# Three weight buffers instead of two, and the second layernorm applied by halves, in a transformer layer on eight cores

## The chip, the cores and the metric

The kernel runs on all 8 cores of one Trainium2 chip. Each core computes one of the eight batch elements from its own copy of x and the same weights; the cores do not exchange anything. The metric is the device time of one launch in microseconds, that of the slowest core.

## What is computed

One pre-norm transformer layer on x of shape (8, 2048, 1024) in float32, with 16 heads of 64 in the attention and a feed-forward part of four hidden products, cut here to its core:

```python
x = x + attn(layernorm(x), wq, bq, wk, bk, wv, bv, wo, bo)   # softmax attention, 16 heads
n = layernorm(x)                                             # over the last axis, eps 1e-5
h = silu(n @ w1.T * s1) * (n @ w2.T * s2)                    # 1024 -> 4096
h = gelu(h @ h1.T * sh1)                                     # 4096 -> 4096
h = gelu(h @ h2.T * sh2)                                     # 4096 -> 4096
x = x + (h @ w3.T * s3)                                      # 4096 -> 1024
```

The change touches the second layernorm and the feed-forward part.

## The kernel before

Everything lies with features on the 128 partitions and the S = 2048 tokens of the core's batch element along the free dimension. KD = 8 chunks of 128 features make up D = 1024, KH = 32 make up the 4096. The program is a row of blocks written out by hand. In a block each engine has its own queue of instructions in program order, and semaphores order the engines (a count that an instruction raises by `then_inc`, and that another engine awaits by `wait_ge`). Between blocks all engines meet at a barrier.

First come the first layernorm and the projections with the attention (to about 1029 us), then the normalisation of the attention, the product with wo, whose result x2 lies in x2buf in float32 and is stored to x2hbm, and the statistics of the second layernorm: the rows of means and of inverse deviations, both in rowbuf2, one partition each. The change begins behind them.

**Second layernorm, application (lines 932 to 957).** A block of its own. TensorE spreads the row of means and the row of inverse deviations over all partitions: four matmuls of 512 columns each with a column of ones, into ps_mrep (line 939) and ps_rrep (line 943). Each takes 4 of the 8 PSUM banks. Then VectorE subtracts and multiplies for each of the 8 chunks k, over all 2048 tokens, from x2buf through xsq2 (float32) into act_bf (bfloat16): 16 operations. They go through the helper vop (line 191 in the profile), which makes each wait for the one before.

**Feed-forward part (lines 959 to 1102).** The list sched holds the units of work. There are two halves of the tokens (hf = 0, 1; THALF = 1024 tokens each). In each half come 32 units of w1, 32 of w2, 32 of h1, 32 of h2 and 8 of w3, so 136 units in a half and 272 in all. A unit i computes 128 output features for 1024 tokens: 16 matmuls of 128x512 for w1 and w2 (8 chunks of input by 2 column blocks), and 64 for h1, h2 and w3. Its weights, 128 x 1024 or 128 x 4096 values, are loaded by POOL's queue from float32 in HBM into bfloat16 in wb0 or wb1, by turns. Its result goes into one of two halves of ps_f.

- POOL (line 992) waits until unit i - 2 is through, then issues the load for unit i (line 993). The loads of units 0 and 1 are issued ahead, in the block of the wo product (lines 798, 799).
- TensorE (line 1022) waits for the load and for the eviction of unit i - 2. At the first unit of each stage (m == 0) it waits for all evictions so far, since every unit of a stage reads all that the stage before wrote.
- ScalarE evicts w1 (silu, into hbufA), h1 (gelu, into hbufA) and h2 (gelu, into hbufB) on line 1042; VectorE evicts w2 (times hbufA, into hbufB, line 1058) and w3 (plus x2, into ostg, line 1069).
- SyncE loads x2 back for w3 and stores the output.

hbufA takes the first 64 KB per partition of the arena. It lies over xsq2 (0 to 16 KB), rowbuf2 (16 to 32 KB) and the first half of x2buf (from 32 KB). Each eviction writes 2 KB of it, so the one of unit m = 8 is the first to write where rowbuf2 was, and that of m = 16 the first where x2buf was. The x2 store has to be through before the evictions begin (s_x2st).

```python
g.wait_ge(s_mm, mm0 + i - 1)
g.dma_start(wb[i % 2][:, 0: kc * 128], src[m]).then_inc(swl[i % 2], 16)
```

Of the kernel before, what the change touches and what calls it, by code (L numbers as in the profile page):

```python
# [6 lines left out]
F32 = mybir.dt.float32  # L7
BF16 = mybir.dt.bfloat16
# [4 lines left out]
B, S, D, H, E, HID = 8, 2048, 1024, 16, 64, 4096  # L13
KD = D // 128
KH = HID // 128
# [35 lines left out]
    "ostg":    (139264, 8192),  # L51
    "wb0":     (148352, 8192),
    "wb1":     (156544, 8192),
}
ARENA_SIZE = 164736


def build_nc():
    nc = bass.Bass("TRN2", target_bir_lowering=False)
# [50 lines left out]
    def arena(name, shape, dtype):  # L110
        off, sz = AR[name]
        esz = 2 if dtype == BF16 else 4
        nbytes = int(np.prod(shape[1:])) * esz
        assert nbytes <= sz, (name, nbytes, sz)
        return nc.alloc_sbuf_tensor_at(name, shape, dtype,
                                       offset=arena_base + off)[:]
# [27 lines left out]
    hbufB = arena("hbufB", [128, KH * THALF], BF16)  # L144
    wb0 = arena("wb0", [128, KH * 128], BF16)
    wb1 = arena("wb1", [128, KH * 128], BF16)
    x2rb = arena("x2rb", [128, 2 * 1024], F32)
    ostg = arena("ostg", [128, 2 * 1024], F32)

# [4 lines left out]
    with es:  # L154
# [10 lines left out]
        s_dcp = es.enter_context(nc.semaphore("s_dcp"))  # L165
        s_wl0 = es.enter_context(nc.semaphore("s_wl0"))
        s_wl1 = es.enter_context(nc.semaphore("s_wl1"))
        s_wc = es.enter_context(nc.semaphore("s_wc"))
        s_mm = es.enter_context(nc.semaphore("s_mm"))
        s_evs = es.enter_context(nc.semaphore("s_evs"))  # L170
# [10 lines left out]
        s_xe = es.enter_context(nc.semaphore("s_xe"))  # L181
        s_dd1 = es.enter_context(nc.semaphore("s_dd1"))

        swl = [s_wl0, s_wl1]
        sxr = [s_xr0, s_xr1]
        sout = [s_o0, s_o1]
        sdd = [s_dd0, s_dd1]
# [1 line left out]
        def vop(v, meth, *a, **kw):  # L189
            v.wait_ge(s_v, n["v"])  # L190
            getattr(v, meth)(*a, **kw).then_inc(s_v, 1)  # L191
            n["v"] += 1
            return n["v"]
# [102 lines left out]
        with nc.Block() as blk:  # L296
            @blk.gpsimd
            def _(g):
                g.dma_start(onescol_bf, onescol_c).then_inc(s_small, 16)
                g.dma_start(bqs, bq_d).then_inc(s_small, 16)  # L300
                g.dma_start(bks, bk_d).then_inc(s_small, 16)
                g.dma_start(bo_sb, bo_d).then_inc(s_small, 16)
                g.dma_start(bvr_sb, bv_d).then_inc(s_small, 16)
                g.dma_start(s1_sb, s1_d).then_inc(s_small, 16)
                g.dma_start(s2_sb, s2_d).then_inc(s_small, 16)
                g.dma_start(sh1_sb, sh1_d).then_inc(s_small, 16)
                g.dma_start(sh2_sb, sh2_d).then_inc(s_small, 16)
                g.dma_start(s3_sb, s3_d).then_inc(s_small, 16)
                g.wait_ge(s_x, 16)
                g.dma_start(wq_sb, wq_d).then_inc(s_wqkv, 16)  # L310
                g.dma_start(wk_sb, wk_d).then_inc(s_wqkv, 16)
                g.dma_start(wv_sb, wv_d).then_inc(s_wqkv, 16)
# [475 lines left out]
        with nc.psum_tensor("ps_sxb", [1, S], F32) as ps_sxb:  # L788
            with nc.psum_tensor("ps_wo", [128, 2 * 1024], F32) as ps_wo:
                with nc.Block() as blk:  # L790
# [4 lines left out]
                    @blk.gpsimd  # L795
                    def _(g):
                        g.wait_ge(s_pe, pe0 + 2 * KD + KD - 1)
                        g.dma_start(wb0[:, 0: KD * 128], w1_d[0]).then_inc(s_wl0, 16)
                        g.dma_start(wb1[:, 0: KD * 128], w1_d[1]).then_inc(s_wl1, 16)

                    @blk.sync
                    def _(sy):
# [122 lines left out]
                        vop(v, "tensor_scalar", rowr, rowr, -0.5, 1.5, ALU.mult, ALU.add)  # L925
                        vop(v, "tensor_mul", rowr, rowt, rowr)

        with (
            nc.psum_tensor("ps_mrepb", [128, S], F32) as ps_mrep,
            nc.psum_tensor("ps_rrepb", [128, S], F32) as ps_rrep,  # L930
        ):
            with nc.Block() as blk:
                @blk.tensor
                def _(t):
                    rowm = rowbuf2[0:1, 0:S]
                    rowr = rowbuf2[0:1, S:2 * S]
                    ins = None
                    for nn in range(4):
                        t.matmul(ps_mrep[:, nn * 512:(nn + 1) * 512], ones_sb,
                                 rowm[0:1, nn * 512:(nn + 1) * 512],  # L940
                                 start=True, stop=True)
                    for nn in range(4):
                        ins = t.matmul(ps_rrep[:, nn * 512:(nn + 1) * 512], ones_sb,
                                       rowr[0:1, nn * 512:(nn + 1) * 512],
                                       start=True, stop=True)
                    ins.then_inc(s_pe, 1)

                n["pe"] += 1

                @blk.vector  # L950
                def _(v):
                    v.wait_ge(s_pe, n["pe"])
                    for k in range(KD):
                        vop(v, "tensor_sub", xsq2[:, (k % 2) * S:(k % 2) * S + S],
                            x2buf[:, k * S:(k + 1) * S], ps_mrep[:])
                        vop(v, "tensor_mul", act_bf[:, k * S:(k + 1) * S],
                            xsq2[:, (k % 2) * S:(k % 2) * S + S], ps_rrep[:])

        wb = [wb0, wb1]
        sched = []  # L960
        for hf in range(2):
            sched += [("w1", hf, m) for m in range(KH)]
# [18 lines left out]
        w3_evv_val = [evv0 + evv_b[i] + 1  # L981
                      for i, (lay, hf, m) in enumerate(sched) if lay == "w3"]

        with nc.psum_tensor("ps_f", [128, 2 * 1024], F32) as ps_f:
            with nc.Block() as blk:
                @blk.gpsimd
                def _(g):
                    for i, (lay, hf, m) in enumerate(sched):
                        if i < 2:
                            continue  # L990
                        src, kc = wsrc[lay]
                        g.wait_ge(s_mm, mm0 + i - 1)  # L992
                        g.dma_start(wb[i % 2][:, 0: kc * 128], src[m]).then_inc(swl[i % 2], 16)  # L993

                @blk.tensor
                def _(t):
                    for i, (lay, hf, m) in enumerate(sched):
                        src, kc = wsrc[lay]
                        t.wait_ge(swl[i % 2], 16 * (i // 2 + 1))
                        if m == 0:  # L1000
                            if evs_b[i] > 0:
                                t.wait_ge(s_evs, evs0 + evs_b[i])
                            if evv_b[i] > 0:
                                t.wait_ge(s_evv, evv0 + evv_b[i])
                        elif i >= 2:
                            lay2 = sched[i - 2][0]
                            if eng[lay2] == "s":
                                t.wait_ge(s_evs, evs0 + evs_b[i - 2] + 1)
                            else:
                                t.wait_ge(s_evv, evv0 + evv_b[i - 2] + 1)  # L1010
                        if lay in ("w1", "w2"):
                            rhs, rb, rstride = act_bf, hf * THALF, S
                        elif lay == "h1":
                            rhs, rb, rstride = hbufB, 0, THALF
                        elif lay == "h2":
                            rhs, rb, rstride = hbufA, 0, THALF
                        else:
                            rhs, rb, rstride = hbufB, 0, THALF
                        ins = None
                        for k in range(kc):  # L1020
                            for nn in range(2):
                                ins = t.matmul(  # L1022
                                    ps_f[:, (i % 2) * 1024 + nn * 512:(i % 2) * 1024 + (nn + 1) * 512],
                                    wb[i % 2][:, k * 128:(k + 1) * 128],
                                    rhs[:, k * rstride + rb + nn * 512: k * rstride + rb + (nn + 1) * 512],
                                    start=(k == 0), stop=(k == kc - 1))
                        ins.then_inc(s_mm, 1)
# [4 lines left out]
                @blk.scalar  # L1032
                def _(sc):
                    sc.wait_ge(s_x2st, 16 * KD)
                    for i, (lay, hf, m) in enumerate(sched):
                        if eng[lay] != "s":
                            continue
                        sc.wait_ge(s_mm, mm0 + i + 1)  # L1038
                        dst = hbufA if lay in ("w1", "h1") else hbufB
                        func = AF.Silu if lay == "w1" else AF.Gelu  # L1040
                        ssb = {"w1": s1_sb, "h1": sh1_sb, "h2": sh2_sb}[lay]
                        sc.activation(dst[:, m * THALF:(m + 1) * THALF],  # L1042
                                      ps_f[:, (i % 2) * 1024:(i % 2) * 1024 + 1024],
                                      func, scale=ssb[:, m:m + 1]).then_inc(s_evs, 1)
                        n["evs"] += 1
# [120 lines left out]
```

## Time and profile before

| | us |
|---|---|
| median of the two timed runs | 4099.9 |
| the two timed runs | 4070.94 and 4128.85 |
| the profiled execution, its own time | 3864.26 |
| its span on the slowest core, from the first to the last instruction | 3862.7 |

| stage in the profiled execution | from, us | to, us |
|---|---|---|
| rows of the second layernorm done | | 1249.9 |
| broadcasts and application of the second layernorm | 1250.2 | 1302.6 |
| w1 and w2, half 0 | 1303.0 | 1570.8 |
| h1, half 0 | 1576.6 | 2023 |
| h2 and w3, half 0 | 2023 | 2577 |
| w1 and w2, half 1 | 2579.2 | 2850.5 |
| h1, h2 and w3, half 1 | 2857.9 | 3862 |

PE is TensorE's matmuls, PEld its loads of weights, DVE is VectorE, ACT is ScalarE, SP is SyncE. PEclk and the granted clock are the share of TensorE's full speed of 2.4 GHz that the chip gave it. In a group the first number behind the bar is the busy time, then comes the mean of one instruction; behind the second bar stands the idle time of that engine just before these instructions, and what ended it. In the chain of waits each piece begins where the one before it ends, and "issue" is time in which nothing shown was waited for. Matmul records overlap, so a pitch is taken from a stretch divided by its count.

### The profile page before, as it was taken

What the parts mean: (1) busy time and instruction counts of PE and PEld (TensorE: products, weight loads), DVE (VectorE), ACT (ScalarE), POOL (GpSimd) and SP (SyncE); (2) the same over time, 40 slices, a digit from 0 to 9 for tenths busy, and PEclk for the clock granted to TensorE, in tenths of its full rate; (3) what the DMA queues carried; (4) which work ended last, traced back from release to release, by engine and by line L of the source; (5) the groups of instructions that cost most, each with busy time, mean ns of one, the idle gap of its engine ahead of it and who ended that gap; (6) DMA issues with size and microseconds to landing.
All of it is one profiled execution on the core that took longest, in us unless ns stands there. A gap on an engine that the chain in (4) does not pass through costs nothing.

```text
span 3862.7 us, 35099 instructions; the slowest of 8 cores (3845.2 to 3862.7 us)
## 1 busy us (share of the span) xinstructions
PE 3384.2 (88%) x14708; PEld 1385.2 (36%) x14708; DVE 479.1 (12%) x453; ACT 805.6 (21%) x741; POOL 151.3 (4%) x290
## 2 busy tenths in 40 slices
PE   2378888888696588999999999998889999999999
PEld 0122222222132233344444444443334444444444
DVE  0522222222222303000000000000210000000000
ACT  1014777777601120000000000002000000000000
POOL 0000000000000011000000000001100000000000
PEclk9589999999868799999999999999999999999999
DMA  6000000001013244444444444454444444444445
GB/s 153 0 1 1 1 1 1 1 1 23 1 62 118 33 63 64 80 76 76 76 76 73 77 76 76 96 127 63 63 74 77 77 77 77 75 76 76 76 71 144
DMA packets 49612, 237.44 MB, mean 61 GB/s; under 512 B 7777, under 2 KB 7842, under 8 KB 28338
## 3 DMA queue, kind: packets, MB, share of 16 engines
q0 software_dynamic: 40176, 193.04, 29.8%
q1 hardware_dynamic: 9282, 42.15, 3.1%
q8 instruction: 120, 1.97, 0.2%
q14 instruction: 34, 0.28, 0.0%
HBM read 411.19 MB, written 16.78 MB: 111 GB/s over the span
## 4 chain that ended last, share of the span: by engine, by line
PE 59%; DMA 5%; issue 1%; ACT 0%; DVE 0%; POOLq 0%; DVEq 0%; ACTq 0%
PE ps_f L1022 59%; DMA wb<-w 5%; DMA wb<-h 0%; ACT hbufA L1042 0%; DVE hbufB L1058 0%; DVE ostg L1069 0%; ACT hbufB L1042 0%; POOLq L992 0%; ACTq L1038 0%; DVEq L1056 0%; DVEq L1055 0%; DVEq L1068 0%; DVEq L1066 0%
## 5 line engine op out<-in xcount | busy, mean ns | idle before, releaser
L1022 PE MATMUL ps_f<-hbufB,wb 128*128 128x512 bf16 x5120 | 1110.8, 380 | 16.1 <-DMA wb<-h 13.2
L1022 PE MATMUL ps_f<-hbufA,wb 128*128 128x512 bf16 x4096 | 884.4, 379 | 3.0 <-ACT hbufA L1042 3.0
L1022 PEld LDWEIGHTS ps_f<-hbufB,wb 128*128 128x128 bf16 x5120 | 501.8, 98 | 625.1 <-issue 24.9
L728 ACT ACTIVATE pbuf<-ps_sc,cneg 128x1024 bf16<-128x1024 f32 x512 | 531.3, 1135 | 268.8 <-PE ps_sc L434 267.5
L1022 PEld LDWEIGHTS ps_f<-hbufA,wb 128*128 128x128 bf16 x4096 | 400.6, 98 | 486.8 <-issue 4.0
L1022 PE MATMUL ps_f<-act_bf,wb 128*128 128x512 bf16 x2048 | 457.4, 381 | 122.2 <-DMA wb<-w 62.1
L1022 PEld LDWEIGHTS ps_f<-act_bf,wb 128*128 128x128 bf16 x2048 | 194.8, 98 | 385.9 <-issue 168.6
L455 PE MATMUL ps_aE<-pbuf,vt_sb 128*65 128x512 bf16 x512 | 220.6, 431 | 86.5 <-DVE q_sb L712 85.3
L1069 DVE SCALAR_TENSOR_TENSOR ostg<-ps_f,s_sb,x2rb 128x1024 f32<-128x1024 f32 x16 | 20.6, 1284 | 1994.0 <-PE ps_f L1022 1994.0
L1042 ACT ACTIVATE hbufB<-ps_f,sh_sb 128x1024 bf16<-128x1024 f32 x64 | 71.4, 1116 | 816.0 <-PE ps_f L1022 816.0
L1042 ACT ACTIVATE hbufA<-ps_f,sh_sb 128x1024 bf16<-128x1024 f32 x64 | 71.4, 1116 | 784.7 <-PE ps_f L1022 784.7
L434 PE MATMUL ps_sc<-q_sb,k_sb 64*128 64x512 bf16 x1024 | 212.8, 406 | 18.6 <-ACT pbuf L728 1.5
L455 PE MATMUL ps_aO<-pbuf,vt_sb 128*65 128x512 bf16 x512 | 208.2, 407 | 0.0
L434 PEld LDWEIGHTS ps_sc<-q_sb,k_sb 64*128 64x128 bf16 x1024 | 58.6, 93 | 262.2 <-issue 262.1
L1058 DVE SCALAR_TENSOR_TENSOR hbufB<-ps_f,s_sb,hbufA 128x1024 bf16<-128x1024 f32 x64 | 82.2, 1284 | 460.5 <-PE ps_f L1022 460.5
L455 PEld LDWEIGHTS ps_aE<-pbuf,vt_sb 128*65 128x65 bf16 x512 | 56.7, 111 | 215.8 <-issue 215.8
L993 POOL DMA_DIRECT2D wb<-h x128 | 67.6, 528 | 1683.6 <-PE ps_f L1022 1651.6
L1042 ACT ACTIVATE hbufA<-ps_f,s_sb 128x1024 bf16<-128x1024 f32 x64 | 71.4, 1116 | 191.9 <-PE ps_f L1022 191.9
L1042 ACT ACT_TABLE_LOAD x4 | 5.1, 1283 | 493.9 <-PE ps_f L1022 493.9
L993 POOL DMA_DIRECT2D wb<-w x142 | 74.9, 528 | 804.1 <-PE ps_f L1022 804.1
L229 PE MATMUL ps_sxa<-xbuf,onescol_sb 128*1 128x512 f32 x64 | 30.6, 623 | 73.5 <-PEq L296 73.5
L771 PE MATMUL ps_rep<-rtile,selpair 16*128 16x512 f32 x64 | 54.9, 1058 | 17.0 <-DVE rtile L191 17.0
(93 smaller groups left out, 1003.2 us busy)
## 6 DMA issues: line engine op xcount, KB each, us to landing
wb<-h POOLq DMA_DIRECT2D x128, 1024.0 KB, 8.1
wb<-w POOLq DMA_DIRECT2D x128, 256.0 KB, 3.8
wb<-w POOLq DMA_DIRECT2D x16, 1024.0 KB, 9.5
xrb<-xst SPq DMA_DIRECT2D x8, 1024.0 KB, 4.8
x2hbm<-x2buf SPq DMA_DIRECT2D x8, 1024.0 KB, 14.2
x2rb<-x2hbm SPq DMA_DIRECT2D x16, 512.0 KB, 9.7
out_fm<-ostg SPq DMA_DIRECT2D x16, 512.0 KB, 8.9
wqld<-wq POOLq DMA_DIRECT2D x1, 2048.0 KB, 16.6
```

Of the source, the lines that this page charges most:

```text
L229: t.matmul(ps_sx[:, nn * 512:(nn + 1) * 512], onescol_sb, src[:, k * S + nn * 512: k * S + (nn + 1) * 512], start=(k == 0), stop=(k == KD ...
L434: ins = t.matmul(ps_sc[:, bufo + hh * TQ: bufo + (hh + 1) * TQ], k_sb[p0:p0 + 64, j * S + c * 128: j * S + (c + 1) * 128], q_sb[p0:p0 + 64 ...
L455: ins = t.matmul(ps_a[:, :], vt_sb[:, vslot: vslot + 65], pbuf[:, sb + hh * TQ: sb + (hh + 1) * TQ], start=(c == 0), stop=(c == TC - 1))
L728: sc.activation(pbuf[:, (c % 4) * 1024:(c % 4) * 1024 + 1024], ps_sc[:, (c % 2) * 1024:(c % 2) * 1024 + 1024], AF.Exp, bias=cneg[:, j:j + ...
L771: ins = t.matmul(ps_rep[:, (j % 2) * S + nn * 512:(j % 2) * S + (nn + 1) * 512], selpair_sb[:, j * 128:(j + 1) * 128], rtile[:, nn * 512:( ...
L993: g.dma_start(wb[i % 2][:, 0: kc * 128], src[m]).then_inc(swl[i % 2], 16)
L1022: ins = t.matmul(ps_f[:, (i % 2) * 1024 + nn * 512:(i % 2) * 1024 + (nn + 1) * 512], wb[i % 2][:, k * 128:(k + 1) * 128], rhs[:, k * rstri ...
L1042: sc.activation(dst[:, m * THALF:(m + 1) * THALF], ps_f[:, (i % 2) * 1024:(i % 2) * 1024 + 1024], func, scale=ssb[:, m:m + 1]).then_inc(s_ ...
L1058: v.scalar_tensor_tensor(hbufB[:, m * THALF:(m + 1) * THALF], ps_f[:, (i % 2) * 1024:(i % 2) * 1024 + 1024], s2_sb[:, m:m + 1], hbufA[:, m ...
L1069: v.scalar_tensor_tensor(ostg[:, (nst % 2) * 1024:(nst % 2) * 1024 + 1024], ps_f[:, (i % 2) * 1024:(i % 2) * 1024 + 1024], s3_sb[:, m:m + ...
```

## The change

Two things are changed.

**Three weight buffers.** wb2 joins wb0 and wb1, with a semaphore s_wl2 of its own. Unit i takes buffer i % 3, its load waits until unit i - 3 is through, and the loads of three units are issued ahead. The list of units, the two halves of ps_f and the evictions stay.

**Layernorm by halves.** The separate block for the application is gone; its work now stands at the head of the feed-forward block, for tokens 0 to 1023 and then for 1024 to 2047. Each half has 4 broadcast matmuls into ps_m2 and ps_r2 (2 banks each, so that they fit beside the 4 banks of ps_f) and 16 VectorE operations on 128x1024. The subtraction now writes act_bf in bfloat16, and the multiplication works in place there; xsq2 is not used for it. The broadcasts of half 1 wait for VectorE's last operation of half 0 (vnh[0]), because they overwrite the same banks. The first w1 unit of a half waits for that half's operations (vnh[hf]). ScalarE waits for the broadcasts of half 1 before the eviction of m = 8, and for the operations of half 1 before that of m = 16, because hbufA lies over rowbuf2 and x2buf.

```diff
@@ @@
                         g.dma_start(wb0[:, 0: KD * 128], w1_d[0]).then_inc(s_wl0, 16)
                         g.dma_start(wb1[:, 0: KD * 128], w1_d[1]).then_inc(s_wl1, 16)
+                        g.dma_start(wb2[:, 0: KD * 128], w1_d[2]).then_inc(s_wl2, 16)
...
-                @blk.vector
-                def _(v):
-                    v.wait_ge(s_pe, n["pe"])
-                    for k in range(KD):
-                        vop(v, "tensor_sub", xsq2[:, (k % 2) * S:(k % 2) * S + S],
-                            x2buf[:, k * S:(k + 1) * S], ps_mrep[:])
-                        vop(v, "tensor_mul", act_bf[:, k * S:(k + 1) * S],
-                            xsq2[:, (k % 2) * S:(k % 2) * S + S], ps_rrep[:])
...
+                for hf_ in range(2):
+                    @blk.tensor
+                    def _(t, hf=hf_):
+                        if hf == 0:
+                            t.wait_ge(s_v, vrows)
+                        else:
+                            t.wait_ge(s_v, vnh[0])
+                        ins = None
+                        for nn in range(2):
+                            t.matmul(ps_m2[:, nn * 512:(nn + 1) * 512], ones_sb,
...
+                        for nn in range(2):
+                            ins = t.matmul(ps_r2[:, nn * 512:(nn + 1) * 512], ones_sb,
...
+                        ins.then_inc(s_pe, 1)
+                        n["pe"] += 1
+                        pe_rep[hf] = n["pe"]
+
+                    @blk.vector
+                    def _(v, hf=hf_):
+                        v.wait_ge(s_pe, pe_rep[hf])
+                        for k in range(KD):
+                            vop(v, "tensor_sub",
+                                act_bf[:, k * S + hf * 1024: k * S + hf * 1024 + 1024],
+                                x2buf[:, k * S + hf * 1024: k * S + hf * 1024 + 1024],
+                                ps_m2[:])
+                            vop(v, "tensor_mul",
+                                act_bf[:, k * S + hf * 1024: k * S + hf * 1024 + 1024],
+                                act_bf[:, k * S + hf * 1024: k * S + hf * 1024 + 1024],
+                                ps_r2[:])
+                        vnh[hf] = n["v"]
...
-                        if i < 2:
+                        if i < 3:
                             continue
                         src, kc = wsrc[lay]
-                        g.wait_ge(s_mm, mm0 + i - 1)
-                        g.dma_start(wb[i % 2][:, 0: kc * 128], src[m]).then_inc(swl[i % 2], 16)
+                        g.wait_ge(s_mm, mm0 + i - 2)
+                        g.dma_start(wb[i % 3][:, 0: kc * 128], src[m]).then_inc(swl[i % 3], 16)
...
-                        t.wait_ge(swl[i % 2], 16 * (i // 2 + 1))
+                        t.wait_ge(swl[i % 3], 16 * (i // 3 + 1))
+                        if lay == "w1" and m == 0:
+                            t.wait_ge(s_v, vnh[hf])
...
+                        if lay == "w1" and hf == 0 and m == 8:
+                            sc.wait_ge(s_pe, pe_rep[1])
+                        if lay == "w1" and hf == 0 and m == 16:
+                            sc.wait_ge(s_v, vnh[1])
```

On TensorE, between the last matmul of the statistics and the fourth w1 unit, the queue before reads as follows (ps_mrepb and ps_rrepb are the spread rows):

```order
L889 MATMUL ps_sqb<-sqbf2_66,onescol_bf 1x512 x3
L872 UNCONDITIONAL_BRANCH
L933 UNCONDITIONAL_BRANCH [waits barrier_Pool_Activation_PE_DVE_SP_release]
L939 MATMUL ps_mrepb<-rowbuf2_67,ones_sb 128x512 x4
L943 MATMUL ps_rrepb<-rowbuf2_67,ones_sb 128x512 x4
L932 UNCONDITIONAL_BRANCH
L995 UNCONDITIONAL_BRANCH [waits barrier_Pool_Activation_PE_DVE_SP_release]
L1022 MATMUL ps_f<-act_bf,wb0_70 128x512 [waits s_wl0]
L1022 MATMUL ps_f<-act_bf,wb0_70 128x512 x15
L1022 MATMUL ps_f<-act_bf,wb1_71 128x512 [waits s_wl1]
L1022 MATMUL ps_f<-act_bf,wb1_71 128x512 x15
L1022 MATMUL ps_f<-act_bf,wb0_70 128x512 [waits s_wl0,s_evs]
```

And the same place in the changed kernel:

```order
L970 UNCONDITIONAL_BRANCH [waits barrier_Pool_Activation_PE_DVE_SP_release]
L978 MATMUL ps_m2<-rowbuf2_67,ones_sb 128x512 [waits s_v]
L978 MATMUL ps_m2<-rowbuf2_67,ones_sb 128x512
L982 MATMUL ps_r2<-rowbuf2_67,ones_sb 128x512 x2
L970 UNCONDITIONAL_BRANCH
L978 MATMUL ps_m2<-rowbuf2_67,ones_sb 128x512 [waits s_v]
L978 MATMUL ps_m2<-rowbuf2_67,ones_sb 128x512
L982 MATMUL ps_r2<-rowbuf2_67,ones_sb 128x512 x2
L1012 UNCONDITIONAL_BRANCH
L1041 MATMUL ps_f<-act_bf,wb0_70 128x512 [waits s_wl0,s_v]
L1041 MATMUL ps_f<-act_bf,wb0_70 128x512 x15
L1041 MATMUL ps_f<-act_bf,wb1_71 128x512 [waits s_wl1]
```

The eight broadcast matmuls are now two groups of four, each behind a wait for VectorE, and both stand ahead of the first w1 unit.

On POOL, before, the loads of the weights up to the second that waits for a unit:

```order
L798 DMA wb0_70<-w1 128x1024 [waits s_pe]
L799 DMA wb1_71<-w1 128x1024
L790 UNCONDITIONAL_BRANCH
L986 UNCONDITIONAL_BRANCH [waits barrier_Pool_Activation_PE_DVE_SP_gather]
L993 DMA wb0_70<-w1 128x1024 [waits s_mm]
L993 DMA wb1_71<-w1 128x1024 [waits s_mm]
```

And in the changed kernel:

```order
L801 DMA wb0_70<-w1 128x1024 [waits s_pe]
L802 DMA wb1_71<-w1 128x1024
L803 DMA wb2_72<-w1 128x1024
L793 UNCONDITIONAL_BRANCH
L1003 UNCONDITIONAL_BRANCH [waits barrier_Pool_Activation_PE_DVE_SP_gather]
L1010 DMA wb0_70<-w1 128x1024 [waits s_mm]
L1010 DMA wb1_71<-w1 128x1024 [waits s_mm]
```

Three loads stand ahead of the barrier instead of two, and those behind it go round three buffers.

## Rows read from the trace of the kernel before

**Rows 1.** Head of the page

```profile
span 3862.7 us, 35099 instructions; the slowest of 8 cores (3845.2 to 3862.7 us)
```

**Rows 2.** Granted clock: die, median span, mean granted clock

```profile
die 0 (median of its cores): 3851.5 us, clock 0.950
```

**Rows 3.** The chain that ended last, by line, share of the span

```profile
PE ps_f L1022 59%; DMA wb<-w 5%; DMA wb<-h 0%; ACT hbufA L1042 0%; DVE hbufB L1058 0%; DVE ostg L1069 0%; ACT hbufB L1042 0%; POOLq L992 0%; ACTq L1038 0%; DVEq L1056 0%; DVEq L1055 0%; DVEq L1068 0%; DVEq L1066 0%
```

**Rows 4.** Groups: busy, mean ns of one | idle before, releaser

```profile
L1022 PE MATMUL ps_f<-hbufB,wb 128*128 128x512 bf16 x5120 | 1110.8, 380 | 16.1 <-DMA wb<-h 13.2
...
L1022 PE MATMUL ps_f<-act_bf,wb 128*128 128x512 bf16 x2048 | 457.4, 381 | 122.2 <-DMA wb<-w 62.1
```

**Rows 5.** The chain in time, start of w1, half 0: start us, us, what

```profile
1303.04 5.05 PE ps_f L1022 x16
...
1308.62 3.84 DMA wb<-w
...
1312.71 3.63 PE ps_f L1022 x16
```

**Rows 6.** DMA issues: count, KB each, median us to landing

```profile
wb<-h POOLq DMA_DIRECT2D x128, 1024.0 KB, 8.1
```

**Rows 7.** Timeline of the layernorm's application: start us, us, engine, line, operation

```profile
1247.65 2.28 DVE L191 TENSOR_TENSOR rowbuf<-xsq,rowbuf 1x2048 f32<-1x2048 f32 x1
...
1250.25 7.16 PE L939 MATMUL ps_mrepb<-rowbuf,ones_sb 1*128 1x512 f32 x8 [22.75 <-PEq L872]
...
1264.41 2.29 DVE L191 TENSOR_TENSOR xsq<-x2buf,ps_mrepb 128x2048 f32<-128x2048 f32 x1 [14.48 <-PE ps_rrepb L943]
1266.80 2.29 DVE L191 TENSOR_TENSOR act_bf<-xsq,ps_rrepb 128x2048 bf16<-128x2048 f32 x1
```

**Rows 8.** VectorE groups before 1250 us, shapes apart; columns as in Rows 4

```profile
L191 DVE SCALAR_TENSOR_TENSOR x2buf<-ps_wo,bo_sb,xrb 128x1024 f32<-128x1024 f32 x16 | 20.5, 1284 | 61.4 <-PE ps_wo L831 61.4
...
L670 DVE TENSOR_TENSOR vt_sb<-ps_x,bvrep 128x1024 bf16<-128x1024 f32 x16 | 19.6, 1227 | 60.4 <-PE ps_x L413 60.4
L191 DVE TENSOR_TENSOR attn_n<-q_sb,ps_rep 128x2048 bf16<-128x2048 bf16 x8 | 18.3, 2288 | 39.4 <-PE ps_rep L771 39.4
```

**Rows 9.** Stretches: us, busy PE, PEld, DVE, ACT, POOL, PEclk, DMA share, GB/s

```profile
1250.30:1264.10 13.80, 13.80 (x16) 5.06 (x16) 0.00 (x0) 0.00 (x0) 0.00 (x0) 0.50 0.00 0
1303.00:1575.00 272.00, 228.50 (x1024) 97.45 (x1024) 41.08 (x32) 37.00 (x33) 33.77 (x64) 0.99 0.45 66
1576.00:2023.00 447.00, 445.06 (x2048) 200.97 (x2048) 0.00 (x0) 37.00 (x33) 16.88 (x32) 0.99 0.43 75
1576.50:1580.00 3.50, 3.44 (x9) 1.24 (x10) 0.00 (x0) 0.00 (x0) 0.00 (x0) 0.50 1.04 152
2023.00:2466.00 443.00, 442.19 (x2048) 200.32 (x2048) 0.00 (x0) 35.21 (x32) 16.55 (x32) 1.00 0.44 76
```

**Rows 10.** Landing of the loads into wb, w1 and w2 of half 1

```profile
DMA to landing us min/median/max: 3.6/3.9/5.7
```

**Rows 11.** The chain in time, into w2 (half 0) and w1 (half 1)

```profile
1438.23 0.02 issue
...
1439.58 7.08 PE ps_f L1022 x32
...
2579.15 3.63 PE ps_f L1022 x16
```

**Rows 12.** Timeline, first h1 matmuls of both halves; idle before in brackets

```profile
1576.56 23.76 PE L1022 MATMUL ps_f<-hbufB,wb 128*128 128x512 bf16 x96 [5.80 <-DMA wb<-h]
...
2857.86 12.33 PE L1022 MATMUL ps_f<-hbufB,wb 128*128 128x512 bf16 x46 [7.36 <-DMA wb<-h]
```

**Rows 13.** The two loads issued ahead

```profile
L798 POOL DMA_DIRECT2D wb<-w x1: 527/527/527, 1200.4 to 1200.4; - x1
...
DMA to landing us min/median/max: 8.9/9.2/9.6
```

More of the change, by code:

```diff
@@ L53 @@
     "wb1":     (156544, 8192),
+    "wb2":     (164736, 8192),
 }
-ARENA_SIZE = 164736
+ARENA_SIZE = 172928
 def build_nc():
@@ L146, in build_nc @@
     wb1 = arena("wb1", [128, KH * 128], BF16)
+    wb2 = arena("wb2", [128, KH * 128], BF16)
     x2rb = arena("x2rb", [128, 2 * 1024], F32)
@@ L167, in build_nc @@
         s_wl1 = es.enter_context(nc.semaphore("s_wl1"))
+        s_wl2 = es.enter_context(nc.semaphore("s_wl2"))
         s_wc = es.enter_context(nc.semaphore("s_wc"))
@@ L182, in build_nc @@
         s_dd1 = es.enter_context(nc.semaphore("s_dd1"))
-        swl = [s_wl0, s_wl1]
+        swl = [s_wl0, s_wl1, s_wl2]
         sxr = [s_xr0, s_xr1]
@@ L926, in _ @@
                         vop(v, "tensor_mul", rowr, rowt, rowr)
[L928 to L948, printed above, removed]
-                @blk.vector
-                def _(v):
-                    v.wait_ge(s_pe, n["pe"])
-                    for k in range(KD):
-                        vop(v, "tensor_sub", xsq2[:, (k % 2) * S:(k % 2) * S + S],
-                            x2buf[:, k * S:(k + 1) * S], ps_mrep[:])
-                        vop(v, "tensor_mul", act_bf[:, k * S:(k + 1) * S],
-                            xsq2[:, (k % 2) * S:(k % 2) * S + S], ps_rrep[:])
-        wb = [wb0, wb1]
+                    vrows = n["v"]
+        wb = [wb0, wb1, wb2]
         sched = []
@@ L982, in build_nc @@
                       for i, (lay, hf, m) in enumerate(sched) if lay == "w3"]
-        with nc.psum_tensor("ps_f", [128, 2 * 1024], F32) as ps_f:
-            with nc.Block() as blk:
+        with (
+            nc.psum_tensor("ps_f", [128, 2 * 1024], F32) as ps_f,
+            nc.psum_tensor("ps_m2", [128, 1024], F32) as ps_m2,
+            nc.psum_tensor("ps_r2", [128, 1024], F32) as ps_r2,
+        ):
+            with nc.Block() as blk:
+                pe_rep = [0, 0]
+                vnh = [0, 0]
+                rowm = rowbuf2[0:1, 0:S]
+                rowr2 = rowbuf2[0:1, S:2 * S]
+                for hf_ in range(2):
[8 more added lines that the diff above has]
+                            t.matmul(ps_m2[:, nn * 512:(nn + 1) * 512], ones_sb,
+                                     rowm[0:1, hf * 1024 + nn * 512: hf * 1024 + (nn + 1) * 512],
+                                     start=True, stop=True)
+                        for nn in range(2):
+                            ins = t.matmul(ps_r2[:, nn * 512:(nn + 1) * 512], ones_sb,
+                                           rowr2[0:1, hf * 1024 + nn * 512: hf * 1024 + (nn + 1) * 512],
+                                           start=True, stop=True)
+                        ins.then_inc(s_pe, 1)
[14 more added lines that the diff above has]
+                        vnh[hf] = n["v"]
@@ L1023, in _ @@
                                     ps_f[:, (i % 2) * 1024 + nn * 512:(i % 2) * 1024 + (nn + 1) * 512],
-                                    wb[i % 2][:, k * 128:(k + 1) * 128],
+                                    wb[i % 3][:, k * 128:(k + 1) * 128],
                                     rhs[:, k * rstride + rb + nn * 512: k * rstride + rb + (nn + 1) * 512],
```

## The prediction

> **What bounds the kernel now.** I read the page's head first, then the chain of waits, then the groups, then stretches. The profiled execution took 3864.3 us, 1.6 us more than its span of 3862.7 us; its eight cores lie within 0.5% of each other, and the mean granted clock of a die is 0.950 [rows 1, 2]. The chain that ended last begins in the feed-forward part and is TensorE work for 59%; the next share, 5%, is "DMA wb<-w", loads of weights [rows 3]. The groups say which weights: the matmuls that read act_bf (stages w1 and w2) have 122.2 us of idle time in front of them, those of h1 and w3, which read hbufB, only 16.1 us for two and a half times as many [rows 4]. So h1, h2 and w3 run at TensorE's pace and w1 and w2 do not.
>
> Why, the chain in order of time shows: a unit of 16 matmuls (3.63 us), 0.53 us until POOL issues the load into the buffer that just came free, 3.84 us until it lands, 0.25 us, and the unit after next starts; so two units take some 8.25 us [rows 5]. With two buffers a load has only one unit to hide behind, and a w unit is shorter than its load. An h unit is four times as long, and its load (8.1 us for four times the bytes) hides [rows 6].
>
> Ahead of this stands the second layernorm's application. The last row operation ends at 1247.65 + 2.28 = 1249.93 us, the first w1 matmul starts at 1303.04: 53.1 us in which TensorE broadcasts two rows (7.16 us the first, 14.2 us both, since VectorE starts at 1264.41) and then waits while VectorE does 16 operations of 2.29 us at a pitch of 2.39 [rows 5, 7]. Nothing lies beside them.
>
> **The change, part A: the layernorm by halves.** On the path are now: the wait and block change as before (to 1250.25), the broadcasts of half 0 (half of 14.2, so 7.1 us, to 1257.4), 0.2 us handover, 16 VectorE operations on 128x1024, and then, because TensorE's queue is in order, the broadcasts of half 1, another 7.1 us behind VectorE's last operation of half 0; the w1 matmuls stand behind these. An operation of 128x1024 with a PSUM and an SBUF operand takes 1.227 us as an addition (the first bound) and 1.284 us as a scalar_tensor_tensor (the other) [rows 8]; I take 1.227, which is the same instruction, plus the gap of 0.10 us between chained operations seen at 2048: 16 x 1.33 = 21.3 us, to 1278.8. That the multiplication now reads bf16 instead of f32 costs nothing by its neighbour: attn_n is made from bf16 and PSUM in 2.288 us per 2048, act_bf from f32 and PSUM in 2.287 [rows 7, 8]. Add 0.2 and 7.1: w1 starts at 1286.1 instead of 1303.04, **16.9 us** gained. With 1.284 us it would be 16.0. The broadcasts ran at a granted clock of 0.50 (the 1.2 GHz level) through all of their 14 us [rows 9]; were half 1's to run at 2.4 GHz they would take 3.5 us less, 20.4 us gained. I keep them slow, and the start of w1 too, as before: its first unit takes 5.05 us, not 3.63 [rows 5].
>
> Half 1's 16 operations (21.3 us) run on VectorE beside w1. VectorE has nothing to do before w2: of the 272 us of w1 and w2 it was busy for 41.1, in 32 operations, the evictions of w2 [rows 9]. ScalarE now waits for them before its 17th eviction, some 58 us after the start of w1 (17 units of 3.46), and before its 9th, at 31 us, for broadcasts that are over by then. Without that cover the 21 us would be paid. The block less saves the 0.47 us handover, counted above.
>
> **Part B: three weight buffers.** A load for unit i is issued when unit i-3 ends, so two units hide it: 2 x 3.455 = 6.9 us against 0.75 + 3.8 us in the median. In half 1 the landings took 3.9 us in the median and 5.7 us at most [rows 10]; with the 0.75 us even the longest fits, at 6.45. TensorE then runs at the pitch of h2, where 2048 matmuls took 442.2 us, 0.2159 us each [rows 9]. For 1024 of them: 221.1 us. What stays: 1.4 us of slow clock at w1's first unit of half 0, and the barrier between w1 and w2, where the first unit waits for the last eviction, 1438.23 to 1439.58, 1.35 us [rows 11]. So 223.9 us in half 0 and 222.5 in half 1. Before, from first matmul to last end: 1303.04 to 1570.77, 267.7 us; 2579.15 to 2850.50, 271.4 us (each end is the start of h's first unit less the idle time ahead of it, 5.80 and 7.36 us) [rows 5, 11, 12]. Gained: 43.8 + 48.9 = **92.7 us**.
>
> The step to h1: its first load is issued one unit (3.455 us) earlier, so the idle 5.8 us become 2.3 and the 7.4 become 3.9; VectorE's last eviction, needed there as well, ends 1.5 us behind the last unit and stays hidden. **6.9 us.** The wait also let the clock drop: 0.50 granted in h1's first 3.5 us [rows 9], though after the 1.35 us at w2 the next 32 matmuls took 7.08 us, the fast pitch [rows 11]. h1 was busy for 445.1 us where h2 was for 442.2 [rows 9]. With 2.3 us of idle time I expect the drop to be gone in half 0 (2.9 us) and keep it in half 1: **2.9 us**, between 0 and 5.1 for both.
>
> POOL issues the same number of loads; the third one is issued ahead, behind the other two at 1201 us. It lands long before it is used (unit 2 starts near 1295); those two took 8.9 and 9.6 us [rows 13]. h1, h2 and w3 gain nothing beyond their first unit: they hardly wait [rows 4].
>
> **The sum.** 16.9 + 92.7 + 6.9 + 2.9 = 119.4 us, so 3864.3 - 119.4 = 3744.9 us for an execution like the profiled one. The two timed runs are another matter: their median is 4099.9 us, 235.6 us above the profiled execution, and the profile cannot say where these lie. If they lie outside the feed-forward part, the whole 119 come off: 3980. If they are a slower TensorE there, its roughly 2450 us became 2686, a mean clock of 0.912; then a unit takes 3.79 us, the old pair 3.98 + 4.62 = 8.60 and the new one 7.58, so the pair gains 1.02 us and not 1.34: over 62 pairs 20 us less, 4000. I forecast the timed median between them, 3990 us, a gain of 110 us or 2.7%.
>
> **Rivals.**
> (1) The timed runs are like the profiled execution this time: 3745 us. Its eight cores show that the chip does this; the two earlier timed runs did not.
> (2) Loads do not overlap one another, and the queue becomes the pace: a unit each 0.25 + 3.84 us, 4.09. Then 128 units lose 0.64 us each to the forecast, 81 us; 38 stay: 3826, or 4062 from the median. For it: before, the load's landing was always nearly over when the next was issued. Against: the two first loads, the second issued 0.53 us behind the first, took 8.9 and 9.6 us, so they landed 1.2 us apart [rows 13], and four times the bytes take 8.1 us and not 15, so most of the 3.8 us is latency [rows 6].
> (3) Half 1's normalisation is not hidden: 21 us back, 3766 or 4011.
> (4) Slower: the granted clock. With w1 and w2 free of gaps TensorE is dense for 2457 us at a stretch, and if the chip then grants less, every stage pays. The point from which it decides: 2457 / (2457 + 119) = 0.954 gives all back; at 0.926 the kernel is over 2% slower; at 0.90 it costs 273 us: 4018 against 3864. For it: something that the profile does not show made the timed runs 6% longer. Against: h1 and h2 keep TensorE busy for 887 of 890 us at a grant of 0.99 and 1.00 [rows 9], and w1 and w2 are only a fifth of the stretch.
>
> The Trainium skill (TensorE: Matmul & The Clock Gate, section Part 1: The HAM clock gate, under Seeing it yourself) has a rule for (4): once three cores of a die run dense matmuls, a current limit takes the die to 13/16 of the clock, and one should budget 1.95 GHz. This trace does not agree: the core shown is granted 0.99 and 1.00 in h1 and h2 while its neighbours run the same stages, within 0.5% of its time [rows 2, 9]. By the rule the new stretch would take 2457 / 0.8125 = 3024 us, 567 more. If the timed runs met it in part before the change as well, that only shrinks the gain.
>
> **How the numbers follow.** Forecast 0.60, (1) 0.22, (2) 0.08, (3) 0.05, (4) 0.05. The range reaches from (1) with its better bounds (3735) to (2) on the median's scale (4062, so 4060); the forecast's own range is 3950 to 4045: the two sums, widened by the 1.4% between the two runs and by the smaller gain at a still lower clock. Over 2% is about what can be told from no change. Forecast, (1) and (3) are faster by more, but at 2.4 to 3.1% and with that scatter 0.07 of them may read as less: faster 0.80, within 2% 0.15 with (2), slower 0.05.
>
> **What would show it.** Right: idle time ahead of the act_bf matmuls near 10 us instead of 122 (beside the wait for the layernorm), no "DMA wb<-w" in the chain, pieces of hundreds of matmuls in w1 and w2 at 0.216 us; w1's first matmul 36 us behind the last row operation; 32 operations of 1.23 us on act_bf, 16 of them beside w1, and no wait of ScalarE for VectorE; 2.3 and 3.9 us ahead of h1. Wrong: loads landing in over 6 us, TensorE waiting for wb; ScalarE waiting at its 17th eviction; a grant under 0.99 in h1 and h2.

## The result and the profile after

| | before | changed |
|---|---|---|
| median of all runs, us | 3872.21 (10 runs, 3859.46 to 4308.43) | 3753.86 (13 runs, 3751.24 to 4026.07) |
| ratio to before | | 0.9711, 95% interval 0.9697 to 0.9725 |

The change makes the kernel 2.9% faster. In some executions of either kernel the cores of one die or of both are granted less clock and the time is longer (up to 4308 us in this table), so the ratio and the times compared below leave such executions out, and of the profiled one here, which is such an execution on cores 4 to 7, only cores 0 to 3 are read.

The cores of that execution, their span and mean granted clock:

```profile
core 2: 3750.7 us, clock 0.950
...
die 0 (median of its cores): 3745.3 us, clock 0.951
die 1 (median of its cores): 3897.8 us, clock 0.903
```

Cores 0 to 3 took 3738.6 to 3750.7 us, close to the table's median of 3754 us, and core 2, the slowest of them, is read below.

The groups of core 2 that answer to [rows 4]:

```profile
L1041 PE MATMUL ps_f<-hbufB,wb 128*128 128x512 bf16 x5018 | 1102.8, 380 | 16.3 <-DMA wb<-h 7.9 <-ACT hbufB L1065 3.0
...
L1041 PE MATMUL ps_f<-act_bf,wb 128*128 128x512 bf16 x2006 | 443.1, 381 | 7.1 <-ACT hbufA L1065 2.8 <-DVE ostg L1092 1.7 <-issue 0.3
```

The idle time ahead of the act_bf matmuls went from 122.2 us to 7.1, and no load of w1 or w2 is left among what ended it. Ahead of the hbufB matmuls the wait for the first loads of h1 fell from 13.2 us to 7.9. The total there still reads 16.3 us, but this trace lacks the records of 102 of core 2's 5120 matmuls (x5018), and each missing one looks like a short pause: core 0, which has all of them, waited 8.0 us for these loads and shows 11.0 in all.

The layernorm's application, the timeline as in [rows 7]:

```profile
1251.08 2.28 DVE L194 TENSOR_TENSOR rowbuf<-xsq,rowbuf 1x2048 f32<-1x2048 f32 x1
...
1253.83 3.75 PE L978 MATMUL ps_m<-rowbuf,ones_sb 1*128 1x512 f32 x4 [22.90 <-PEq L876]
...
1257.38 3.62 PE L982 MATMUL ps_r<-rowbuf,ones_sb 1*128 1x512 f32 x4
...
1261.17 1.22 DVE L194 TENSOR_TENSOR act_bf<-x2buf,ps_m 128x1024 bf16<-128x1024 f32 x1 [7.81 <-PE ps_r L982]
1262.49 1.22 DVE L194 TENSOR_TENSOR act_bf<-act_bf,ps_r 128x1024 bf16<-128x1024 bf16 x1
...
1282.41 3.75 PE L978 MATMUL ps_m<-rowbuf,ones_sb 1*128 1x512 f32 x4 [21.42 <-DVE act_bf L194]
...
1285.95 3.62 PE L982 MATMUL ps_r<-rowbuf,ones_sb 1*128 1x512 f32 x4
...
1289.75 1.22 DVE L194 TENSOR_TENSOR act_bf<-x2buf,ps_m 128x1024 bf16<-128x1024 f32 x1 [7.48 <-PE ps_r L982]
1289.90 10.28 PE L1041 MATMUL ps_f<-act_bf,wb 128*128 128x512 bf16 x34 [0.33 <-issue]
```

The last row operation ends at 1253.36 us. Four broadcasts take 7.2 us, VectorE's operations stand at a pitch of 1.325 us and last until 1282.3, the next four broadcasts take 7.2 us more, and w1 starts at 1289.90, beside VectorE's first operation of half 1: 36.5 us where it was 53.1.

From w1 to w2 in the chain of waits (to compare with [rows 11]), and then from w2 to h1:

```profile
1403.23 1.12 ACT hbufA L1065
...
1404.49 8.36 PE ps_f L1041 x38
```

```profile
1508.80 9.96 DMA wb<-h
...
1519.11 8.28 PE ps_f L1041 x26
```

The only stop between w1 and w2 is ScalarE's eviction. Into h1 the load still ends the wait, and it took 9.96 us to land.

The stretches of core 2 (w1's first 3 us, the next 4, w1 and w2 of half 0, h1 and h2 of half 0), with the columns of [rows 9]:

```profile
1289.90:1293.00 3.10, 3.10 (x8) 1.17 (x8) 2.89 (x3) 0.00 (x0) 0.00 (x0) 0.50 0.00 0
1293.00:1297.00 4.00, 4.00 (x14) 1.52 (x13) 3.69 (x4) 0.83 (x1) 0.36 (x1) 0.69 0.00 0
1290.00:1514.00 224.00, 221.59 (x999) 100.25 (x1019) 59.09 (x47) 36.94 (x33) 33.40 (x63) 0.99 0.51 74
1517.00:1964.00 447.00, 442.53 (x2007) 200.95 (x2048) 0.00 (x0) 35.92 (x33) 16.43 (x31) 0.99 0.45 78
1964.00:2407.00 443.00, 439.58 (x2006) 200.32 (x2048) 0.00 (x0) 35.55 (x32) 16.97 (x32) 1.00 0.43 76
```

w1 starts at a grant of 0.50, as before, and has 0.69 in the next 4 us. Of 224 us TensorE is busy for 221.6. VectorE's 59 us are the evictions of w2 and most of half 1's normalisation.

The second half, in TensorE's timeline: w1's first matmuls, and h1's (in brackets the idle time before):

```profile
2521.41 110.67 PE L1041 MATMUL ps_f<-act_bf,wb 128*128 128x512 bf16 x502 [1.74 <-DVE ostg L1092]
...
2748.17 12.03 PE L1041 MATMUL ps_f<-hbufB,wb 128*128 128x512 bf16 x54 [3.96 <-DMA wb<-h]
```

From 2521.41 to the end of w2 at 2748.17 - 3.96 = 2744.21 us are 222.8 us, where it was 271.4.

### The profile page after: what moved, and what is told of

Its sections match the earlier page's. It is cut to its first block, busy times and chain, and to the rows that moved or that the text cites. A ratio compares the mean times of both kernels' runs of the same rounds, so it can differ in the third digit from the quotient of the medians.

```text
span 3930.6 us, 34871 instructions; the slowest of 8 cores (3738.6 to 3930.6 us)
## 1 busy us (share of the span) xinstructions
PE 3537.6 (90%) x14453; PEld 1433.1 (36%) x14708; DVE 481.5 (12%) x469; ACT 804.9 (20%) x741; POOL 151.3 (4%) x290
## 4 chain that ended last, share of the span: by engine, by line
PE 66%; DMA 1%; DVE 1%; issue 1%; ACT 0%; DVEq 0%; ACTq 0%; POOLq 0%
PE ps_f L1041 66%; DVE act_bf L194 1%; DMA wb<-h 0%; PE ps_m L978 0%; PE ps_r L982 0%; ACT hbufA L1065 0%; DMA wb<-w 0%; DVE ostg L1092 0%; ACT hbufB L1065 0%; DVEq L193 0%; ACTq L1057 0%; POOLq L1009 0%; DVEq L1091 0%; DVEq L1089 0%; DVEq L1079 0%
## 5 line engine op out<-in xcount | busy, mean ns | idle before, releaser
L1041 PE MATMUL ps_f<-hbufB,wb 128*128 128x512 bf16 x5018 | 1201.7, 404 | 15.8 <-DMA wb<-h 5.8
L1041 PE MATMUL ps_f<-hbufA,wb 128*128 128x512 bf16 x4014 | 926.8, 393 | 8.0 <-ACT hbufA L1065 2.9
L1041 PEld LDWEIGHTS ps_f<-hbufB,wb 128*128 128x128 bf16 x5120 | 524.9, 103 | 692.6 <-issue 345.2
L1041 PEld LDWEIGHTS ps_f<-hbufA,wb 128*128 128x128 bf16 x4096 | 411.8, 101 | 522.9 <-issue 159.5
L1041 PE MATMUL ps_f<-act_bf,wb 128*128 128x512 bf16 x2006 | 475.3, 400 | 7.6 <-ACT hbufA L1065 2.8
L1041 PEld LDWEIGHTS ps_f<-act_bf,wb 128*128 128x128 bf16 x2048 | 208.5, 102 | 275.4 <-issue 121.3
```

Source lines behind the costliest of these rows:

```text
L1041: ins = t.matmul(ps_f[:, (i % 2) * 1024 + nn * 512:(i % 2) * 1024 + (nn + 1) * 512], wb[i % 3][:, k * 128:(k + 1) * 128], rhs[:, k * rstri ...
```

## The experiments

Each version was run four to six times, on one of two chips. Its ratio is to runs of before in the same job, whose medians were 3861.6, 3861.7 and 3864.7 us. Where a version is set against the changed kernel, that is its 3753.9 us from the table above, unless the text says "in the same job". The trace lines are of the slowest core where no core is named.

**Three buffers alone.** The kernel before with the first part of the change, so the layernorm is one block again.

```diff
+    "wb2":     (164736, 8192),
...
-                        g.wait_ge(s_mm, mm0 + i - 1)
-                        g.dma_start(wb[i % 2][:, 0: kc * 128], src[m]).then_inc(swl[i % 2], 16)
+                        g.wait_ge(s_mm, mm0 + i - 2)
+                        g.dma_start(wb[i % 3][:, 0: kc * 128], src[m]).then_inc(swl[i % 3], 16)
```

> The kernel before with three weight buffers alone; the layernorm stays one block. Theory (the gain is the sum of two independent parts, 92.7 + 6.9 + 2.9 us from the loads and 16.9 us from the halves): about 3862 - 101 = 3761 us, ratio to before 0.974; idle ahead of the act_bf matmuls falls from 122 us to about 45 (the layernorm's 39 us and the barriers). Rival (the halves are needed for the loads' gain, because w1's first units start cold and late, or VectorE and the loads share something): less than 90 us, above 3772 us.

Measured: 3768.4 and 3771.2 us, ratio 0.9765 (0.9741 to 0.9788), some 92 us less than before. TensorE's waits in the whole of what follows the statistics:

```profile
PE ps_f L1026 <- PEq L936: 38.8, 1, 38.8
...
PE ps_f L1026 <- DMA wb<-h: 8.4, 2, 4.4
```

The layernorm's 38.8 us stand as before, and no wait for a load of w1 or w2 is in the list. So the loads' gain does not need the halves. The size fits neither expectation well: 101 us was the theory's (its terms add up to 102.5), under 90 the rival's, and 92 is nearer the rival's bound. Where the theory's missing 9 us are, the trace of this run's slowest core shows: its first broadcast starts 3.9 us later than before's (1254.19 and 1250.25 us), h1's first load took 10 us to land here too, so its waits are 8.4 us and not 6.2, w1 and w2 took 1.6 us more than forecast, and the clock was down at h1 of half 0 (0.67 granted in its first 3.5 us), where the theory had no drop.

**Halves alone.** The changed kernel with two weight buffers.

```diff
-                        g.wait_ge(s_mm, mm0 + i - 2)
-                        g.dma_start(wb[i % 3][:, 0: kc * 128], src[m]).then_inc(swl[i % 3], 16)
+                        g.wait_ge(s_mm, mm0 + i - 1)
+                        g.dma_start(wb[i % 2][:, 0: kc * 128], src[m]).then_inc(swl[i % 2], 16)
```

> The changed kernel with two weight buffers again; the layernorm by halves alone. Theory: 17 us less than before, about 3845 us, ratio 0.9956; w1's first matmul 36.5 us behind the last row operation; load waits in w1 and w2 as before. Rival (with half of the layernorm beside w1, VectorE's 16 operations disturb the POOL queue's loads or w1's pace): nothing gained, 3855 us or more, and landings in w1 above 4 us.

Measured: 3842.2 to 3845.9 us, median 3845.2, ratio 0.9958 (0.9943 to 0.9973). That is 16.5 us gained, as expected. TensorE's waits, then the landings of the first five loads of w1, four of them issued while VectorE's operations of half 1 ran, and those of the loads behind them:

```profile
PE ps_f L1037 <- DMA wb<-w: 60.0, 65, 2.1
...
PE ps_f L1037 <- DMA wb<-h: 10.4, 2, 7.5
```

```profile
DMA to landing us min/median/max: 3.7/3.8/3.9
```

```profile
DMA to landing us min/median/max: 3.6/3.8/4.5
```

The waits for loads are back (60.0 us for w1 and w2, 62.1 before), and a load beside VectorE lands as fast as one without it. The two parts add up: 92 and 16.5 are 108 us, and the whole change takes the 3863 us of before to 3754, 109 less.

**Three buffers without the lead.** One number is changed in the changed kernel.

```diff
-                        g.wait_ge(s_mm, mm0 + i - 2)
+                        g.wait_ge(s_mm, mm0 + i - 1)
```

> The changed kernel, three buffers, but the load of unit i waits for unit i - 2 as before: a third buffer without the longer lead. Theory (what pays is the second unit of lead over the load): all of the loads' gain is gone, the time of the halves alone, about 3845 us. Rival (a third buffer pays by itself, since a load no longer writes the buffer that the unit just ended has read): near the changed kernel, 3754 us.

Measured: 3847.4 us, ratio 0.9964 (0.9948 to 0.9980).

```profile
PE ps_f L1041 <- DMA wb<-w: 50.6, 49, 1.8
...
PE ps_f L1041 <- DMA wb<-h: 15.2, 2, 7.6
```

The third buffer is there and is used by turns, and all that it brought is gone. The waits are near those of two buffers (60.0 and 10.4 us). So it is the load's head start over its unit that pays.

**Nothing hidden.** The first w1 unit waits for half 1's normalisation as well.

```diff
-                            t.wait_ge(s_v, vnh[hf])
+                            t.wait_ge(s_v, vnh[1])
```

> The changed kernel with the first w1 unit of half 0 waiting for the layernorm of half 1 too. Theory (VectorE's 16 operations of half 1 are wholly hidden, and nothing else of the halves is): 21.3 us more than the changed kernel, about 3775 us, which is also 4 us more than a layernorm in one block would give. Rival (part of the gain of the halves comes from the fewer barrier or from shorter operations, not from the overlap): less than 17 us more, below 3771 us.

Measured: 3774.6 and 3776.9 us, ratio 0.9780 (0.9757 to 0.9804), 21 to 23 us more than the changed kernel. TensorE's timeline from half 1's last broadcasts to w1:

```profile
1289.52 3.62 PE L982 MATMUL ps_r<-rowbuf,ones_sb 1*128 1x512 f32 x4
1314.55 5.63 PE L1041 MATMUL ps_f<-act_bf,wb 128*128 128x512 bf16 x19 [21.42 <-DVE act_bf L194]
```

The 21.42 us are the price of the 16 operations when nothing lies beside them, and the time moved by as much.

**h1's first load in two parts.**

```diff
+                        if lay == "h1" and m == 0:
+                            c0 = 2048
+                            g.dma_start(wb[i % 3][:, 0:c0], src[m][:, 0:c0]).then_inc(s_h1a, 16)
...
+                            if two and k == 16:
+                                t.wait_ge(swl[i % 3], 16 * (i // 3 + 1))
```

> The changed kernel with the load of h1's first unit cut in two (columns 0 to 2047, then the rest, each with a semaphore); TensorE starts when the first part is there. Theory (the 3.95 us ahead of h1 are the rest of a 10 us landing, and the wait drops the clock): the idle time falls to VectorE's last eviction, 1.7 us, and h1 starts at full clock: 2 x 2.2 us and 2 x 2 to 3 us, together 8 to 10 us less than the changed kernel, about 3745 us. Rival (the clock falls at such a pause anyway, or the two parts land together): 0 to 4 us less.

Measured: 3745.7, 3745.8 and 3747.3 us, some 8 us less than the changed kernel, ratio to before 0.9701 (0.9673 to 0.9729). The two ratios' intervals overlap, so the 8 us rest on the runs themselves (none of the changed kernel's is under 3751.2) and on the traces. The chain into h1 of half 0:

```profile
1515.63 1.29 DVE hbufB L1093
...
1517.06 5.77 PE ps_f L1053 x26
```

VectorE's last eviction ends the wait now, and the first 26 matmuls take 5.77 us where they took 8.28. All eight cores wait 1.6 us in both halves and start h1 at a grant of 1.00. The spans of cores 0 to 3, which lay between 3739 and 3751 us before this edit, lie between 3738 and 3742, and those of cores 4 to 7 between 3739 and 3744.

**Half 1's broadcasts behind the third unit.**

```diff
                         ins.then_inc(s_mm, 1)
+                        if i == 2:
+                            emit_rep(t, 1)
```

> The changed kernel with half 1's broadcasts behind the third w1 unit instead of ahead of the first. Theory (they cost 7.3 us at the slow clock ahead of w1, and half of that beside matmuls at full clock): w1 starts 7.3 us earlier and pays 3.6 us later, 3.7 us less than the changed kernel, about 3750 us; the broadcasts of half 1 take 3.5 us. Rival (these matmuls with one row drop the clock wherever they stand): no gain or a loss, 3754 us or more.

The first four runs took 3751.6, 3752.9, 3771.4 and 3828.2 us and settled nothing. It was run again, beside the changed kernel itself:

> Half 1's broadcasts behind the third w1 unit once more, since the first look left 3751.6 to 3762 us. Theory, with the stretch from half 0's broadcasts to the start of the fourth unit 2 to 3 us shorter in that trace: 2 to 3 us less than the changed kernel in the same job. Rival: no difference.

> The changed kernel itself, on the chip and in the job of the two others: 3753 to 3754 us, and ahead of h1 on each pair of neighbouring cores (0 and 1, 2 and 3, 4 and 5, 6 and 7) one core with a wait near 2 us and one near 4 us, if the pairing seen in three kernels is a property of the chip.

Measured: 3754.3 to 3755.4 us in four runs and 3791.8 in one more, against 3754.3 to 3755.8 for the changed kernel in the same job, so no difference. TensorE's timeline of core 3:

```profile
1255.84 3.75 PE L976 MATMUL ps_m<-rowbuf,ones_sb 1*128 1x512 f32 x4 [22.90 <-PEq L876]
...
1284.42 12.84 PE L1045 MATMUL ps_f<-act_bf,wb 128*128 128x512 bf16 x48 [21.42 <-DVE act_bf L194]
1297.18 1.98 PE L976 MATMUL ps_m<-rowbuf,ones_sb 1*128 1x512 f32 x4
1299.00 3.24 PE L980 MATMUL ps_r<-rowbuf,ones_sb 1*128 1x512 f32 x4
1302.17 102.29 PE L1045 MATMUL ps_f<-act_bf,wb 128*128 128x512 bf16 x464
1405.82 110.67 PE L1045 MATMUL ps_f<-act_bf,wb 128*128 128x512 bf16 x512 [1.36 <-ACT hbufA L1071]
```

The broadcasts of half 1 take 5.0 us (1297.18 to 1302.17) instead of 7.2, and from the first broadcast to the fourth unit are 46.3 us. In the changed kernel's trace these are 49.4 (1253.83 to the piece that starts at 1303.47, less one matmul). But on this core the 3 us are spent again before w2: from the first broadcast to w2's first matmul are 150.0 us (1255.84 to 1405.82), and in the changed kernel's trace of the same job the eight cores took 149.1 to 150.1. Stretches of core 3 during and behind the late broadcasts, then one of core 2 behind them, with the columns of [rows 9]:

```profile
1297.20:1299.00 1.80, 1.80 (x5) 0.83 (x5) 0.00 (x0) 1.12 (x1) 0.53 (x1) 1.00 0.13 22
1299.00:1302.00 3.00, 3.00 (x5) 0.85 (x3) 0.00 (x0) 0.00 (x0) 0.00 (x0) 0.56 0.52 87
1302.00:1305.00 3.00, 3.00 (x8) 1.02 (x8) 2.44 (x2) 0.00 (x0) 0.00 (x0) 0.50 0.00 0
```

```profile
1298.40:1301.40 3.00, 3.00 (x16) 1.35 (x14) 2.71 (x3) 0.47 (x1) 0.02 (x1) 1.00 0.00 0
```

The grant was 1.00 when these broadcasts began and fell to 0.50 in or just behind them on six cores, on core 3 with TensorE busy throughout; on cores 2 and 6 it stayed at 1.00. Only cores 1, 2 and 6 reach w2 earlier than in the changed kernel, at 147.6, 146.4 and 146.2 us from the first broadcast; the other five take 150.0 to 150.3, and the slowest core makes the time. So the rival's effect is there on most cores and the theory's 3.7 us on two. What decides between them was not tested.

**Both edits.**

> Both of the last two edits. Theory: the two gains add up, 12 to 14 us less than the changed kernel, about 3741 us, ratio to before 0.9685. Rival: one of them gives nothing, 3745 to 3750 us.

Measured: 3743.8 to 3746.6 us, median 3744.5, ratio to before 0.9696 (0.9677 to 0.9715). That is 9 us less than the changed kernel, the fastest version here, where 12 to 14 were expected. Against the split load alone it is 1.3 us, and the two ranges touch; the medians of the eight spans in the two profiled executions are 2.5 us apart (3738.6 and 3741.1). In this trace four cores reach w2 146.1 to 147.6 us after the first broadcast and the other four after 149.9 to 150.3, so most of the later broadcasts' 3.7 us is missing on the slower half, and the runs hardly tell a gain.

**Twice the traffic.** Each load of w1 and w2 in half 0 goes a second time, into ostg, which holds nothing yet.

```diff
+                            g.dma_start(twin[:, q * 1024:(q + 1) * 1024], src[m]).then_inc(s_du[q], 16)
```

> The changed kernel with every load of w1 and w2 in half 0 issued a second time, into an unused place, right behind the first: twice the load traffic there (some 150 instead of 75 GB/s), the same lead. Theory (most of a landing is latency, loads overlap, and two units of lead leave 2.4 us to spare): the landing of the real load stays under 6 us, w1 and w2 of half 0 take 225 us as before, at most 3 us more in all, 3754 to 3757 us. Rival (loads follow one another at 3.8 us each): 7.7 us a unit instead of 3.46, some 260 us more, above 4000 us.

Measured: 3762.6 us in one of six runs, 8 us more than the changed kernel in the same job; the other five took 3816 to 4216 us. On core 2, the landings in half 0, and TensorE's waits for them:

```profile
DMA to landing us min/median/max: 3.8/5.9/7.7
```

```profile
PE ps_f L1051 <- DMA wb<-w: 6.8, 11, 1.4
```

At 146 GB/s, twice the load of the change, a landing takes 5.9 us in the median and 7.7 at most. The waits stay at 6.8 us in all, where loads in single file would have cost 260. The theory's "at most 3 us" was too little: the head start of two units covers the change's own traffic, and at twice that traffic it no longer covers every load.

## Why the prediction was right, and where it was wrong

**The level was wrong.** The step that failed is the last one of the sum, "I forecast the timed median between them, 3990 us". The two runs that I took for the kernel's level, 4070.9 and 4128.9 us, were not it: with eight more runs the median of before is 3872 us, within 0.3% of the profiled execution, and six of the eight lie between 3859 and 3881 us. The result belongs to rival (1), 3745 us, which I gave 0.22. The stated range held 3753.9, but only because it reached down to that rival: the forecast lay 236 us above the result and 118 above even the median of before. What I could have weighed: the eight cores of the profiled execution agreed with each other within 0.5%, and two runs 1.4% apart did not. Why those two runs were long stays open, since the clocks of their cores are not on record; so does the side guess that their 236 us were a slower TensorE in the feed-forward part. That the forecast gain of 110 us is so near the measured 109 is luck: it is a mean of two sums, and the working behind it said 119.

**The working was right in its mechanisms and 10 us too generous** (119.4 us forecast, 109 measured). Its terms can be checked on core 2, whose span is 112 us under that of before's slowest core:

| term | forecast, us | measured, us |
|---|---|---|
| last row operation to w1 | 36.2 | 36.5 |
| w1 and w2, half 0 | 223.9 | 225.3 |
| wait ahead of h1, half 0 | 2.3 | 3.95 |
| slow clock in h1, half 0 | 0 | 2.5 |
| w1 and w2, half 1 | 222.5 | 222.8 |
| wait ahead of h1, half 1 | 3.9 | 3.96 |
| slow clock in h1, half 1 | 2.2 | 0 |
| span | 3743.3 | 3750.7 |

(225.3 is 1519.11 - 3.95 - 1289.90. 2.5 is 8.28 us for 26 matmuls less the 5.77 us that they took after the split load. The forecast span is 3862.7 - 119.4.) The terms differ by 4.0 us together; 3.4 us more come from ahead of the change, where this core's row operations ended at 1253.36 us and not at 1249.93. The cores scatter by such amounts there, and the slowest one is read. The 1.4 us too many in w1 and w2 of half 0 stand at the start of w1: the slow clock lasted beyond the first unit (0.69 granted in the 4 us behind the first 3), so w1 took 113.23 us where w2 took 110.67, 2.6 us more and not 1.4.

**Part A** held in each step: broadcasts slow, 16 operations at 1.33 us (1.325), everything of half 1 hidden. The halves alone gave 16.5 us where I had 16.9, and the price of losing the cover was 21.4 where I had 21.3.

**Part B** held too. Rival (2), loads in single file, is out: with the traffic doubled, two loads were issued in each unit of 3.5 us and took 5.9 us each to land, so they overlap. Rival (3) is out by the timeline, which has VectorE done near 1311 us, some 40 us before ScalarE's 17th eviction, which waited for TensorE alone. Rival (4) did not happen: h1 and h2, and now w1 and w2 too, were granted 0.99 and 1.00 on core 2. The Trainium skill's rule on the current limit, 13/16 of the clock once three cores of a die run dense matmuls (TensorE: Matmul & The Clock Gate, section Part 1: The HAM clock gate), fits these rows no better than it fitted [rows 9], since cores 0, 1 and 3 ran the same stages beside it.

**Mis-sized** was the step to h1 in half 0. My 2.3 us rest on the landing that one core had shown there, 8.36 us, although in half 1 the same trace has 9.92. It is 9.96 here and 10.05 with three buffers alone, so the wait was 3.95 us, and the clock fell after all: the 2.9 us that I took for half 0 did not come there. With the load split neither amount was left, on any core.

## What to carry to other kernels

When units of work are shorter than the landing of their data, count the units of head start, not the buffers: with the third buffer and the old wait nothing was gained. A load four times as large at a stage boundary needs more head start than its neighbours, or a cut, so that work begins on its first part. A gain seen between two marks in one core's trace is in the time only if it is still there at the end of the stage, on the slowest core. And before tying a forecast to two timed runs, compare them with the profiled execution: here the runs were 1.4% apart, its cores 0.5%, and its time was the level.

## What had not been expected of the hardware

The waits ahead of h1 come in pairs. In the changed kernel's second trace cores 0, 2 and 4 waited 2.4, 2.1 and 1.9 us in half 0, and their neighbours 1, 3 and 5 waited 4.3, 4.8 and 4.7 (cores 6 and 7 were closer together, 3.7 and 2.7); with three buffers alone it was 2.0 and 1.8 beside 4.0 and 4.0 on the first die. That was expected of this run from the ones before it, on every pair, and came out on three of four. The core that waits longer has the longer landing. The chain of waits, first of core 0, then of core 1:

```profile
1506.36 8.41 DMA wb<-h
```

```profile
1509.16 10.34 DMA wb<-h
```

Core 1 waits 1.9 us longer for the same 1 MB. Each core's times count from its own first instruction, so which of the two issued its load first can't be read from them. I read it as two neighbours sharing a path to memory, but no run took one of them away, so the cause stays open.

After waits of nearly the same length the clock had fallen or had not: core 2 of the changed kernel was granted 0.50 in the 3.5 us behind a wait of 3.95 us in half 0, and 1.00 behind one of 3.96 us in half 1. In the second trace core 2 was granted 1.00 behind 2.11 us and 0.53 behind 2.13. After waits of 1.4 to 1.8 us it never was down, on any core looked at. The late broadcasts above are a third case: there the grant fell on core 3 without any wait.
